# ALiBi attention, channel attention and experts of a two-layer decoder: three stages with barriers between them become one program

## The reference

```python
x = x + attn(ln(x))                    # layer 0: 16 heads of 128, MXFP4 weights
x = x + cross(ln(x), ctx)              # layer 0: rope, RMS norm, 4 kv heads
x = x + ffn(ln(x))                     # layer 0: gated, 2:4 sparsified hidden
x = x + alibi(ln(x))                   # layer 1: 16 heads of 16, 4 kv heads, causal, ALiBi slopes
x = x + channel(ln(x), ctx)            # layer 1: below
x = x + experts(ln(x))                 # layer 1: below

# channel: q (x), k = v (ctx) are (32, 64, 256); 16 heads of 4 "tokens" each, which act as channels
q = qkv.reshape(bs * 16, 4, 256); k = v = y.reshape(bs * 16, 4, 256)
weight = softmax(einsum('bct,bcs->bts', q * s, k * s))     # 512 matrices of 256 x 256
a = einsum('bts,bcs->bct', weight, v)

# experts: a router over 32 experts, top 8; the last four choices are sent to a primary expert
# where the similarity is at least 0.5; then all 32 experts on all tokens, weighted by combine
for e in range(32):
    g, u = split(x @ gate_up[e].T); y += (silu(g) * u) @ down[e].T * combine[:, e]
```

## Time and profile before

| | us |
|---|---|
| median of 3 runs (lowest to highest) | 1994.62 (1993.47 to 1998.78) |
| the profiled execution's own time | 1999.79 |
| its span, first to last instruction | 1997.6 |
| PE busy, DVE busy | 1700.9 (85%), 1510.0 (76%) |
| ACT busy, POOL busy | 1031.7 (52%), 712.7 (36%) |
| mean granted TensorE clock | 0.953 |

### The profile page before, as it was taken

The page is one execution under the profiler, slowest core; times in us unless marked ns, Lnnn a source line. Parts: engine busy times, 40 slices in busy tenths (PEclk is TensorE's granted clock), DMA queues, the critical chain, the costliest instruction groups (busy, mean ns, idle before and its releaser), DMA issues. The chain is left out here.

```text
span 1997.6 us, 43307 instructions
## 1 busy us (share of the span) xinstructions
PE 1700.9 (85%) x15744; PEld 1000.6 (50%) x15744; DVE 1510.0 (76%) x2875; ACT 1031.7 (52%) x2056; POOL 712.7 (36%) x935
## 2 busy tenths in 40 slices
PE   5999999599999999899747737777777599999998
PEld 2666665267777777745434412222222246656565
DVE  5766666689989899668859969888899268675754
ACT  3666666255555555344336726777778333323222
POOL 4644321586777667313433343434431000000000
PEclk9999999799999999999979978999999799999999
DMA  9601100100000000000001112322321012222221
GB/s 240 166 28 49 28 7 2 62 14 9 15 10 12 6 9 1 1 1 1 1 29 41 37 27 74 83 80 83 95 67 39 23 41 94 88 69 70 67 77 53
DMA packets 87661, 94.91 MB, mean 48 GB/s; under 512 B 17568, under 2 KB 63264, under 8 KB 87456
## 3 DMA queue, kind: packets, MB, share of 16 engines
q1 hardware_dynamic: 83712, 87.76, 15.8%
q10 hardware_dynamic: 2976, 2.32, 0.5%
q0 software_dynamic: 768, 2.10, 0.3%
HBM read 78.51 MB, written 10.22 MB: 44 GB/s over the span
## 5 line engine op out<-in xcount | busy, mean ns | idle before, releaser
L205 PE MATMUL ps<-arena 128*128 128x512 f16 (+6 forms) x6464 | 1091.1, 324 | 57.2 <-DVE arena L1800 14.0
L205 PEld LDWEIGHTS ps<-arena 128*128 128x128 f16 (+1 forms) x6464 | 603.7, 99 | 444.7 <-issue 41.7
L1477 DVE TENSOR_REDUCE arena<-ps 128x4 f32<-128x1024 f32 x256 | 305.0, 1218 | 46.4 <-PE ps L1390 46.4
L1460 ACT ACTIVATE arena<-ps 128x512 f32<-128x512 f32 x512 | 278.4, 597 | 107.4 <-PE ps L1398 87.3
L1390 PE MATMUL ps<-arena 31*128 31x256 f16 x1024 | 107.1, 288 | 106.5 <-ACT arena L1460 47.0
L1445 PE MATMUL ps<-arena 128*32 128x256 f32 x2048 | 170.8, 407 | 2.4 <-ACT arena L1467 0.6
L2221 DVE TENSOR_TENSOR arena<-ps,arena 128x512 f32<-128x512 f32 x96 | 66.2, 690 | 118.7 <-ACT arena L2094 90.6
L2094 ACT ACTIVATE arena<-ps 128x512 f32<-128x512 f32 x96 | 57.2, 596 | 184.7 <-PE ps L205 184.4
L1390 PEld LDWEIGHTS ps<-arena 31*128 31x128 f16 x1024 | 34.8, 93 | 228.4 <-DVE arena L1477 132.7
L968 POOL TENSOR_TENSOR arena<-arena 128x512 f32<-128x512 f32 x96 | 98.7, 1041 | 44.8 <-DVE arena L156 43.7
L1398 PE MATMUL ps<-arena 32*128 32x256 f16 x1024 | 104.8, 284 | 1.5 <-ACT arena L1460 0.4
(11 more groups left out here) (199 smaller groups left out, 2911.8 us busy)
## 6 DMA issues: line engine op xcount, KB each, us to landing
arena<-moe_cw SPq DMA_DIRECT2D x64, 192.0 KB, 2.9
arena<-moe_cw SPq DMA_DIRECT2D x64, 128.0 KB, 3.0
arena<-in_L_ffn_gate_up_proj SPq DMA_DIRECT2D x16, 384.0 KB, 3.6
ch_out<-arena SPq DMA_DIRECT2D x32, 128.0 KB
arena<-moe_cw SPq DMA_DIRECT2D x64, 64.0 KB, 2.8
ch_keys<-arena SPq DMA_DIRECT2D x48, 64.0 KB, 2.0
arena<-ch_keys SPq DMA_DIRECT2D x64, 48.0 KB
arena<-arena SPq DMA_DIRECT2D x192, 16.0 KB
```

The lines of the kernel that those rows point to most:

```text
L205: last = nc.tensor.matmul(out, a, b, start=start and n == 0, stop=stop and n == len(pairs) - 1, skip_group_check=not group)
L1460: nc.scalar.activation(pT[:, b % 3, g], ps[:, T[n % len(T)], :].rearrange("p (u t) -> p u t", u=KD), ACT.Exp, scale=CH_SCALE).then_inc(s_e ...
L1477: nc.vector.tensor_reduce(m[:, half % 2, 2 * half_pair:2 * half_pair + 2, j, :], ps[:, bank(user):bank(user) + 2, :].rearrange("p g (u s) ...
```

## The change

The three last stages become one block (`together`); each stage function returns its five lists (`Programs`), and pieces of one stage's list are called from another's.

- ALiBi: POOL clears the channel stage's `qp` and `vz` (`ahead.clear`: memsets of 128x4096 and 128x2048, and four small ones) right behind the 128x8192 memset of the key rows. In its last full pass DVE settles tiles 0 to 7 and POOL normalises and splits tiles 0 and 1. SP loads keys and values of tiles 0 and 1 from its fourth context tile on, and 12 query rows for each of the tiles 0 and 1 near its end. In the draining pass, units 5 to 7, PE and DVE run half steps 0 to 3 of the channel stage. That pass of DVE is unrolled for it.
- Channel: starts at half step 4; DVE settles tiles 8 to 15 at half step 12. SP's `load_v` moves from the end of a tile's list to behind `load_max(2n-1)` and its weight load, one iteration later; SP loads the router's constants at n = 3, POOL prepares them at tile 4. `keys.load` also waits for its predecessor.
- Experts: at half steps 261, 263, 265, 266, 267, behind the last scores, PE turns x of step 0 (into two banks that the scores no longer use) and computes gate and up of units 0 and 1; ACT copies the turned x among its last exponentials; DVE settles tiles 0 to 11 after the last maximum. The channel stage's last two `invert`, three `measured` and the settling of tiles 12 to 15 go to units 2, 8, 9, 12 and 13 of DVE's expert list. PE's router product of step 0 waits for the last output copy of the channel stage, since both use bank 7.
- Memory: the regions are laid out anew so that tiles of neighbouring stages don't overlap in use; sizes, counts of buffers (18 held `h`) and shapes stay.
- `measure` raises a semaphore, and `settle` waits for it.

```diff
+def together(core, *stages):
+    with core.nc.Block() as block:
+        @block.sync
+        def _(sp):
+            for stage in stages:
+                stage.sync(sp)
+        ...
-def settle(core, dve, name):
+def settle(core, dve, name, layer, tiles=range(TILES)):
     nc = core.nc
+    dve.wait_ge(core.measured, TILES * layer + tiles[-1] + 1)
...
 # channel_stage, SP
-            load_v(0)
-            sp.wait_ge(s_zero, 1)
-            for tile in range(2):
-                load_q(tile, range(CH_KEYROWS))
-            load_v(1)
+        for c in keys.stored:
+            sp.wait_ge(c, 48 * TILES // 2)
             for n in range(TILES + 3):
                 if 0 <= 2 * n - 1 < CH_HALVES:
                     load_max(2 * n - 1)
                 stage(2 * n - 1)
+            if 2 <= n + 1 < TILES:
+                load_v(sp, n + 1)
+            if n == 3:
+                moe.load_constants(sp)
                 if 0 <= 2 * n - 3 < CH_HALVES:
                     store_out(2 * n - 3)
...
                     load_out(n - 2)
-                if n + 2 < TILES:
-                    load_v(n + 2)
...
+    def tensor(pe):
+        for n in range(CH_AHEAD, 2 * CH_SLOTS + CH_C_LAG):
+            if n in CH_MOE_STEPS:
+                moe.ahead.tensor(pe, CH_MOE_STEPS.index(n))
+            tensor_step(pe, n)
...
+                if (b, g) == (CH_SLOTS - CH_HALF, 1):
+                    moe.ahead.scalar(act)
...
+    def vector(dve):
+        for n in range(CH_AHEAD, 2 * CH_SLOTS + 1):
+            vector_step(dve, n)
+            if n == CH_SETTLE:
+                settle_tiles(dve, range(TILES // 2, TILES))
+        settle(core, dve, "moe_first", 4, range(TILES - SUBS))
+    def vector_rest(dve, k):
+        if k < 2:
+            invert(dve, TILES - 2 + k)
+        else:
+            measured(dve, TILES - 5 + k)
+        if k == 4:
+            settle(core, dve, "moe_last", 4, range(TILES - SUBS, TILES))
 # alibi_stage
+            if n in (TILES - 2, TILES - 1):
+                sp.wait_ge(ahead.s_zero, 1)
+                ahead.load_q(sp, n - TILES + 2, range(CH_KEYROWS))
...
+                if not alive(0):
+                    for n in ALIBI_CHANNEL[t]:      # [(), (), (), (), (), (0, 1), (2,), (3,)]
+                        ahead.tensor(pe, n)         # and ahead.vector(dve, n) on DVE
+                if isinstance(i, int) and i == STEPS - 1 and t == 0:
+                    ahead.settle(dve, range(TILES // 2))
...
             nc.gpsimd.memset(keys.rows, 1.0).then_inc(s_ones, 1)
+        ahead.clear(pool)
...
+                if i == STEPS - 1 and t in (2, 6):
+                    ahead.norm(pool, t // 4)
 # moe_stage
+    def turn_bank(j, c):
+        return U[c] if j == 0 else R
+    def tensor_ahead(pe, k):
+        if k == 0:
+            for t in (1, 2):
+                turn_route(pe, 0, t)
+        else:
+            if k == 1:
+                pe.wait_ge(s_xlo, KD)
+            n, half = (k - 1) // 2, (k - 1) % 2
+            project(pe, n, half * P, (G, U)[half], (s_gate, s_up)[half])
...
+            if n in MOE_CHANNEL_REST:               # (2, 8, 9, 12, 13)
+                channel().rest(dve, MOE_CHANNEL_REST.index(n))
```

More of the change, by code:

```diff
@@ L1253, with channel_stage @@
 CH_KEYS_AHEAD = 2
-def channel_stage(core, keys, jobs=(), first=0):
+CH_AHEAD, CH_SETTLE = 4, 12
+CH_MOE_STEPS = (2 * CH_SLOTS + 5, 2 * CH_SLOTS + 7, 2 * CH_SLOTS + 9, 2 * CH_SLOTS + 10, 2 * CH_SLOTS + 11)
+@dataclass
+class ChannelAhead:
+    clear: Any
+    norm: Any
+    s_zero: Any
+    load_q: Any
+    load_v: Any
+    settle: Any
+    tensor: Any
+    vector: Any
+    k_in: Any
+    rest: Any
+    outputs_kept: Any
+def channel_stage(core, keys, moe, jobs=(), first=0):
     nc, ps = core.nc, core.ps
@@ new lines, in gpsimd, with split @@
+    def gpsimd(pool):
+        def split(half):
+            split_weights(core, pool, jobs[half:half + 1], first + half, core.own)
+        moe.clear(pool)
+        for tile in range(TILES + 3):
+            if tile + 2 < TILES:
+                norm(pool, tile + 2)
+            if tile == 4:
+                moe.set_up(pool)
+            if 0 <= 2 * tile - 1 < len(jobs):
+                split(2 * tile - 1)
+            if tile < TILES:
+                set_v(pool, 2 * tile)
+            if 2 * tile < len(jobs):
+                split(2 * tile)
+            if 0 <= tile - 2 < TILES:
+                finish(pool, tile - 2)
+            if tile < TILES:
+                set_v(pool, 2 * tile + 1)
@@ L1592, in jobs, with alibi_stage @@
         return out
-def alibi_stage(core, w, keys):
+def alibi_stage(core, w, keys, channel):
     nc, ps = core.nc, core.ps
@@ L1859 @@
 MOE_CHUNK = 768
+MOE_HELD_IN = (1, 8, 5, 4)
+MOE_HELD = sum(MOE_HELD_IN)
+MOE_CHANNEL_REST = (2, 8, 9, 12, 13)
 class MoeWeights:
@@ L2279, in build @@
         with core.stage():
-            alibi_stage(core, alibi, keys)
-        with core.stage():
-            channel_stage(core, keys, later[2], first[2])
-        with core.stage():
-            moe_stage(core, moe)
+            last = []
+            last.append(moe_stage(core, moe, lambda: last[1].ahead))
+            last.append(channel_stage(core, keys, last[0], later[2], first[2]))
+            last.append(alibi_stage(core, alibi, keys, last[1]))
+            together(core, *reversed(last))
 def constants():
```

1497 lines of the change are left out of this document (756 added, 741 removed).

## The result

The changed kernel takes 1948.32 us (median of 4 runs, 1947.09 to 1948.46); the kernel before takes 1994.45 (4 runs, 1993.47 to 1998.78). The ratio is 0.9762, its 95% interval 0.9747 to 0.9777: 46 us faster, where 55.6 had been forecast. The profiled execution after has a span of 1946.7 us and took 1948.45, at its median. The one before took 1999.79, 5.2 above its median. So between the two profiles 50.9 us of span went, and of the miss of 9.3 us about half (4.7) is in my terms. The rest is that the execution I built the sum on was a long one; where its 5 us probably lay is argued at the end of the part on the prediction.

What follows compares the result with a forecast made beforehand. DVE was taken to bound ALiBi and PE the expert stage, with dead seams and late SP rows in the channel stage. Terms -22.2 + 4.9 + 6.3 - 20 - 25.4 + 0.8 = -55.6 gave 1939.0 us, range 1927 to 1955.

Steps and rivals of the forecast that it cites:

- ALiBi to channel: Border of ALiBi and channel stages: rows loaded early and half steps 0 to 3 done in the drain; gain 22.2 us.
- Clears at ALiBi's start: ALiBi's head: POOL's moved memsets hold up DVE's settling steps, and all of ALiBi stands behind them; cost 4.9 us.
- Settling inside the stages: DVE's settling moved into stages: 3.3 us in ALiBi's last full pass, 3.0 at half step 12; cost 6.3 us.
- the rule's second place: Settling meets POOL's arithmetic within a pass: three such steps each wait up to 1.0 us; 3 us worse.
- The free ones: Settlings after the channel stage's last maximum and at expert unit 13: no cost, or 3.4 us for the latter if not.
- SP's list: Channel stage: moved value load cuts SP's loop from 22.8 to 20.0 us; 4 us of stops left, gain 20.
- Rival A: Channel stage: SP's loop stays the bound and the gain there is 8 to 12 us; 1949 us, chance 0.17.
- D: Channel stage: SP's 5.0 us wait for POOL comes on top of the loop in 12 tiles; 2019 us, chance 0.03.
- Channel to experts: Border into the expert stage: channel tail ends at 1567.0, unit 2 begins at 1569.5 instead of 1594.9; gain 25.4 us.
- Expert stage: Up to the step 0 weights at PE's unit 11: DVE has two invert and one measured more; cost 0.8 us.
- my own sign of being wrong: Two of three terms, the two stage borders and SP's list in the channel stage, missing by over 5 us.
- the other signs: Included channel turns of 20.7 us throughout, and unit 2 within 3 us of the channel's last product without low clock.

Runs made afterwards that it cites:

- the last kernel: Against the changed kernel: second settling's Newton steps on GpSimd, only transposes in the tail, early clears on ScalarE, key-row memset as 32-bit words; 1932.80 us.

## Why the prediction was right, and where it was not

1. *ALiBi to channel.* 22.2 said, 23.4 measured. DVE had 4.6 us more in the drain and the drain grew by about 1.0, not 2.3: nearly all was hidden. Of the two sources that the term has, the half steps done ahead give about 3.5 of it. The rest is that the rows are loaded and nothing stands in front of the first half step any more.
2. *Clears at ALiBi's start.* 4.9 said, 4.95 measured, and moving them to another engine gave it back. The rule of the Trainium skill ("SBUF — State Buffer", "Who interferes with whom") agrees in kind: the hold goes with GpSimd's instruction and moves to whichever `tensor_scalar` meets it (3.62 in the normalise), and ScalarE's writes of the same bytes cause none. What I left out is the clock. PE was at the low level for one more group of products (2.42 us instead of 1.35 for 24), and the stretch as a whole has 0.90 where it had 0.93: the offset went from +5.3 to +7.1 ahead of the second settling. That is 1.8 us the sum has no term for (0.3 had come from the stage ahead). Whether the longer start did it is open: the three kernels whose second normalise is 14.0 us behind the first aggregation had 1.35 in that group, the eight with 16.2 to 18.9 us had 2.42, but so had the last kernel with its 9.6.
3. *Settling inside the stages.* In ALiBi 2.7 for 3.3. At half step 12 4.5 for 3.0: L197 took 1.55 us there, not 0.2, and ended with an operation of GpSimd's arithmetic. This is the rule's second place, which I had priced and kept out of the sum; it was right at this one. The free ones were free. The two rows:

```profile
1194.08 1.64 POOL L179 TENSOR_TENSOR arena<-arena 128x768 f16<-128x768 f32 x1
...
1194.19 1.55 DVE L197 TENSOR_SCALAR arena<-arena 128x8 f32<-128x8 f32 x1
```

4. *SP's list.* 20 said, 23.3 measured (offset -9.2 to -32.5), 24.8 alone on the kernel before. By the medians it is 19.7 alone and 16.5 in the joined kernel; before's long execution probably adds to the larger figures (below). The loop did get shorter than a tile: nearly all tiles take 20.66 us, and from `store_out` to `load_total` it took 3.84 us where I had 3.6. I kept 4 us of stops back and 1.5 came. Rival A is out. So is D: SP does wait for POOL, 3.6 us ahead of the value load and `store_out`, and nothing behind it is urgent.
5. *Channel to experts.* 25.4 said, 22.7 measured. The tail grew by 7.9 instead of 5.2. The work put in was sized right: PE is busy 6.5 us more (20.76 against 14.26), as said. The step that failed is the one on slack: I let PE's idle time in the tail fall from 2.5 to 1.3 us, and it rose to 3.9. Of that, 2.1 are waits that the sum has no term for: the transposes waited 0.76 for the settling's normalise and the first product 1.34 for `x_lo`. The other gaps only went from 2.5 to 1.8, as PE and ACT take turns: a product between two turned scores leaves ACT without work, 7.8 us in 6 waits where before it had 0.6 in 2. I never asked whether putting the products there pays. It doesn't: without them the kernel is 3.6 us earlier at the next transposes, 1.7 of it clock. The gain of this border is the missing barrier and the early settling, not the overlap.

```profile
1525.39 1.09 ACT L1533 ACTIVATE arena<-ps 128x512 f32<-128x512 f32 x2 [1.74 <-PE ps L1465]
```

6. *Expert stage.* 0.8 said, 4.3 measured; this is the largest miss. The 48 products of units 2 to 5 ran at clock 0.86: 1.7 us. They stand behind a tail of short matmuls and a stall of 1.11 for the table load, but so they do in the four kernels where they took 10.53, so neither is the cause. I had said that no low stretch would be left. At the first L2158 PE waits 2.76 us where before it waited 1.33: DVE has the channel's last `invert` (0.55) and a `measured` (0.43) among the router's steps, and its step L2316 took 1.80 us where before it took 1.22, beside POOL's last `finish`. Together that is about 1.4. The last 1.2 are small pieces.

In all: 0.3 + 1.8 ahead of the settlings, -0.6 and +1.5 in the two, -1.2 and -3.3 for the first border and the list, +2.7 and +3.5 for the second border and the experts, which is 4.7. The mechanisms of parts 1 and 4 were right, and that of part 5 but for the slack; none of the three missed by over 5 us, my own sign of being wrong. But 9.8 us of misses one way met 5.1 the other, and that they cancel so far is luck. Of the other signs, unit 2 did start 2.4 us behind the channel's last product, while the stretch behind it was not free of the low clock.

What stays open: where the 5 us of before's profiled execution lie, and what decides whether PE's clock falls behind a given wait. For the first, the record leaves one place, by elimination: the channel stage between its first and last turn. Everywhere else this profile is as long as that of the kernel with the list alone, within 1.8 us in each of four stretches (1653.4 us in all against 1655.0). Its mean clock of 0.953 is one at which other executions of this kernel took 1993.2 to 1994.9 us. And the kernel after with the old list waits 18.0 us for rows of maxima in 11 times, where this one waits 22.9 in as many. That is argued; a second profile of the kernel before would be needed to show it. For the second, the same wait of 2.54 us ahead of the last 684 products was followed by 112.66 us in after and in three of its variants, and by 110.98 in six. (Clock and wait stand in one place of the trace; that the one causes the other was not tried.)

## What to carry to other kernels

When two stages are joined, price the barrier, the loads and the settling apart from the overlap: here they were nearly all of both borders' gain, and the overlap gave about 3.5 us at one and cost about 2 at the other. Insert foreign matmuls only where no other engine waits for the next matmul; a gap between two engines that take turns is not slack. Look through an in-order queue's list for an item that waits ahead of one that is ready: moving one load in the list was worth 16 to 20 us by the medians.

## What the hardware showed that I had not expected

GpSimd's memset time goes by elements, not bytes: 128x8192 of 16 bits took 6.92 us, the same bytes as 128x4096 of 32 bits 3.51. While it runs, a `tensor_scalar` of 0.2 us on VectorE beside it lasts until it ends. The 16 aggregations beside the same memset take 1.17 us, no more than at the expert stage's start, and ScalarE's 1.86 us writes hold nothing up. PE's granted clock varies where no edit is near: between the kernels the same 684 products came out at 112.66 or 110.98 us, 48 at 12.22 or 10.53, 24 at 2.42 or 1.35. It varies between executions of one kernel as well: nine of the kernel before on one chip went from 1987.3 us at a mean clock of 0.958 to 1997.4 us at 0.948. So one variant can be 1 to 4 us better than another with no cause in its edit.
